# Norm, logits and choice of two routed feed-forwards made chunk by chunk inside the self-attentions in front

## Chip, cores, metric

The kernel runs on 1 core of one Trainium2 chip. The metric is the device time of one execution in microseconds (us), the median over runs.

## The reference

A Perceiver-like network of four layers, each of cross-attention, self-attention and feed-forward on x (128 x 32 tokens of 128 channels, float32), `x = x + f(layernorm(x))` each. Three feed-forwards are mixtures of 8 experts. Those that matter here, cut:

```python
# layer 1 (c_moe): two experts a token, capacity 1280, exact gelu
logits = xt @ w_g;  top_v, top_i = top_k(logits, 2);  probs = softmax over the two
rank = cumsum of the choices over all first choices, then all second ones
h = gelu(x_e @ c_fc[e]);  out = sum over the two of probs * (rank < cap) * (h @ c_proj[e])
# layer 3 (u_moe): one expert a token, behind the attention inside the same sublayer
x = x + attention(rmsnorm(x));  h2 = rmsnorm(x);  top1 = argmax(h2 @ Wr + br)
u = h2 @ W1[e] + b1[e];  y = (u1 * sigmoid(u2)) @ W2[e] + b2[e];  return x + y
```

## The kernel before, in words

X (or `inner`) holds all 4096 tokens in SBUF as 32 tiles of 128 tokens; a chunk is 4 tiles (TPC), there are 8 (CHUNKS). Each sublayer is a block of five instruction streams (SP, POOL, TensorE, ScalarE, VectorE) written out by hand, with semaphores between them and a barrier at its end; only then does the next block's SP fetch its weights.

`self_attention` walks steps s. Step s does the scores of tile s, the weighted values of tile s-2, and work of a chunk at a fixed place: `chunk_at(s, place)` is the chunk c with s = 4c + place. c_self does a cross-attention (s = 0..31) and a self-attention (32..63) in one block of 64 tiles; u_self has 32 tiles with rotary embeddings and a norm of queries and keys (powers at place -3). PSUM bank T_BANK holds a tile's turned weights, O_BANK its outputs. Chunk c of X is ready (`add`, L793) at s = 4c + 9; the base (bias, L407) is added on POOL at 4c + 5.

`routed_experts` is c_moe and u_moe (and a_moe, in layer 0). Its front, for all 32 tiles in two halves: statistics (VectorE), deviation (POOL, L1474), apply (ScalarE, L1653, 4 rows a chunk), turn and logits (TensorE, L1522, L1530), choice and places (VectorE, from L1317), then `put`: POOL scatters each tile's rows by an indirect DMA (L1491) into a DRAM buffer ordered by expert (`slots`), K rows a token. Then SP loads 3 expert tiles at a time (x_slots), TensorE turns them (L1592) and runs `up` (L1606), `turn_hidden` (L1614), `down` (L1623); SP stores the results and POOL gathers them (L1502), VectorE combining (L1907). The second half is scattered during the loop, one transfer a tile. c_moe leaves the combining of its second half to the cross-attention behind (e_cross: gather L2249, combine L2554, four a turn of eight batches in the first eight of 16 turns). Capacity ranks and, in u_moe, `X + base` (L1837) are computed before the loop.

## Time and profile before

| | us |
|---|---|
| median of 3 runs (lowest, highest) | 4197.6 (4193.25, 4206.71) |
| profiled execution: time, span | 4199.95, 4198.1 |
| TensorE, VectorE, ScalarE, POOL busy | 3526.1, 2777.6, 2386.5, 2482.7 |
| mean granted TensorE clock | 0.919 of full |

Busy time is the sum over all sublayers; each has a limit of its own, so the stretches further down matter more. A timeline row gives the start, the length, the engine, the line, output and input, and in brackets the idle time before it and who ended it.

### The profile page before, as it was taken

The numbers are of one execution on the slowest core, as the hardware profiler recorded it, in microseconds if no ns is written. First come the engines' busy times: TensorE is split into PE (matmuls) and PEld (weight loads), VectorE is DVE, ScalarE is ACT, GpSimd is POOL, SyncE is SP. The second block draws the span as 40 slices with busy tenths as digits, with TensorE's granted clock in tenths as the row PEclk, the third lists the DMA queues.
The fourth block names the chain that finished last, engine by engine and source line by source line (L and its number), as shares of the span: only waits on it lengthen the run. The fifth ranks groups of instructions, "written<-read, shape, count | busy, mean of one in ns | idle before, by whom it ended". The sixth has DMA issues, their size and how long they took to land. (4 is left out here: it accounts for less than half of the span.)

```text
span 4198.1 us, 119554 instructions
## 1 busy us (share of the span) xinstructions
PE 3526.1 (84%) x44673; PEld 2462.6 (59%) x44674; DVE 2777.6 (66%) x6958; ACT 2386.5 (57%) x5931; POOL 2482.7 (59%) x2841
## 2 busy tenths in 40 slices
PE   7999959999999759798498999988589999786866
PEld 5666636666666547455366666654356666453444
DVE  6888856666666433477344998876778888663655
ACT  6777725555555424277223777764567777553633
POOL 6666656666666543466433777655456666755733
PEclk9999979999999869889699999998689999887968
DMA  2101010000000112100122111110011011000023
GB/s 69 37 32 37 27 66 5 7 10 10 5 7 2 48 54 77 50 29 24 62 74 64 41 40 40 33 53 17 2 38 37 32 37 32 2 2 6 2 83 94
DMA packets 90544, 145.87 MB, mean 35 GB/s; under 512 B 10112, under 2 KB 66816, under 8 KB 89664
## 3 DMA queue, kind: packets, MB, share of 16 engines
q1 hardware_dynamic: 79936, 119.72, 8.9%
q0 software_dynamic: 10240, 20.99, 1.6%
q8 instruction: 261, 4.28, 0.4%
q14 instruction: 107, 0.88, 0.1%
HBM read 109.61 MB, written 31.06 MB: 34 GB/s over the span
## 5 line engine op out<-in xcount | busy, mean ns | idle before, releaser
L2230 POOL TENSOR_TENSOR t_cross_E<-t_cross_E,t_cross_inverse 128x1028 f32<-128x1028 f32 x128 | 243.4, 1902 | 165.2 <-DVE t_cross_inverse L2512 165.2
L2230 POOL TENSOR_TENSOR a_cross_E<-a_cross_E,a_cross_inverse 128x1028 f32<-128x1028 f32 x128 | 243.3, 1901 | 157.4 <-DVE a_cross_inverse L2512 157.4
L2230 POOL TENSOR_TENSOR e_cross_E<-e_cross_E,e_cross_inverse 128x1028 f32<-128x1028 f32 x128 | 243.6, 1903 | 138.1 <-DVE e_cross_inverse L2512 137.7
L3063 PE MATMUL l_psum<-l_ffn_w,l_hidden 128*128 128x128 f32 x1536 | 218.1, 285 | 32.3 <-POOL l_hidden L2936 32.2
L3063 PEld LDWEIGHTS l_psum<-l_ffn_w,l_hidden 128*128 128x128 f32 x1536 | 190.7, 192 | 70.6 <-POOL l_hidden L2936 43.7
L3056 PE MATMUL l_psum<-l_hT,l_ffn_w 128*128 128x512 f32 x384 | 204.4, 635 | 1.0 <-ACT l_hT L3120 0.9
L2500 DVE TENSOR_REDUCE t_cross_negtop<-t_cross_psum 128x2 f32<-128x514 f32 x256 | 165.5, 688 | 50.0 <-PE t_cross_psum L2314 48.4
L2500 DVE TENSOR_REDUCE a_cross_negtop<-a_cross_psum 128x2 f32<-128x514 f32 x256 | 165.2, 687 | 40.2 <-PE a_cross_psum L2309 39.5
L2500 DVE TENSOR_REDUCE e_cross_negtop<-e_cross_psum 128x2 f32<-128x514 f32 x256 | 164.9, 685 | 37.4 <-PE e_cross_psum L2309 36.7
L2936 POOL TENSOR_TENSOR l_hidden<-l_hidden,l_less 128x512 f32<-128x512 f32 x96 | 122.2, 1295 | 93.3 <-ACT l_hidden L3144 93.3
L3217 DVE TENSOR_TENSOR inner<-l_psum,inner 128x512 f32<-128x512 f32 x48 | 33.2, 692 | 213.0 <-PE l_psum L3048 213.0
L2915 POOL TENSOR_SCALAR l_normed<-inner,l_moments,l_rstd 128x128 f32<-128x128 f32 x192 | 160.3, 845 | 14.8 <-POOL l_rstd L2909 14.8
L2926 POOL TENSOR_TENSOR l_q<-l_q,l_q_stat 128x512 f32<-128x512 f32 x48 | 50.8, 1059 | 183.5 <-DVE l_q_stat L3197 183.5
L2367 PE MATMUL e_cross_psum<-const_sb,e_cross_E 128*128 128x128 f32 x1024 | 135.4, 276 | 2.7 <-POOL e_cross_E L2230 2.1
L2367 PE MATMUL t_cross_psum<-const_sb,t_cross_E 128*128 128x128 f32 x1024 | 134.6, 275 | 2.1 <-POOL t_cross_E L2230 2.1
L2367 PE MATMUL a_cross_psum<-const_sb,a_cross_E 128*128 128x128 f32 x1024 | 133.9, 274 | 2.2 <-POOL a_cross_E L2230 2.1
L2435 ACT ACTIVATE t_cross_kT<-t_cross_psum,t_cross_weights 128x257 f32<-128x257 f32 x128 | 61.1, 477 | 127.4 <-PE t_cross_psum L2293 127.4
L3040 PEld LDWEIGHTS l_psum<-l_qT,l_ctx 32*32 32x32 f32 x6144 | 65.5, 107 | 115.6 <-issue 109.9
L2435 ACT ACTIVATE e_cross_kT<-e_cross_psum,e_cross_weights 128x257 f32<-128x257 f32 x128 | 61.0, 477 | 122.6 <-PE e_cross_psum L2293 122.6
L2435 ACT ACTIVATE a_cross_kT<-a_cross_psum,a_cross_weights 128x257 f32<-128x257 f32 x128 | 61.0, 477 | 120.9 <-PE a_cross_psum L2293 120.9
L2452 ACT ACTIVATE e_cross_E<-e_cross_psum,e_cross_negtop 128x257 f32<-128x257 f32 x256 | 118.8, 473 | 13.4 <-DVE e_cross_negtop L2500 13.2
L2367 PEld LDWEIGHTS e_cross_psum<-const_sb,e_cross_E 128*128 128x128 f32 x1024 | 116.6, 143 | 5.8 <-POOL e_cross_E L2230 2.7
(757 smaller groups left out, 11811.4 us busy)
## 6 DMA issues: line engine op xcount, KB each, us to landing
a_cross_context<-context SPq DMA_DIRECT2D x32, 546.0 KB, 3.5
e_cross_context<-context SPq DMA_DIRECT2D x32, 546.0 KB, 3.5
t_cross_context<-context SPq DMA_DIRECT2D x32, 546.0 KB, 3.5
u_moe_weights<-pack_u_moe SPq DMA_DIRECT2D x1, 5633.0 KB
slots<-l_blank SPq DMA_DIRECT2D x6, 832.0 KB, 12.1
a_moe_x_slots<-slots SPq DMA_DIRECT2D x26, 192.0 KB
slots<-a_moe_y_slots SPq DMA_DIRECT2D x26, 192.0 KB
c_moe_x_slots<-slots SPq DMA_DIRECT2D x26, 192.0 KB
```

Source lines behind the costliest of these rows:

```text
L2230: pool.tensor_tensor(E[:, n % N], E[:, n % N], spread(inverse[:, n % 4], SK, 2), ALU.mult).then_inc(s_unit, 1)
L2367: last = pe.transpose(psum[:, (T_BANK, K_BANK)[c], g * P:(g + 1) * P], E[:, n % N, g, c * P:(c + 1) * P], ident)
L2435: act.activation(kT[:, n % 2], psum[:, K_BANK, 0:SK], ACT.Identity, bias=w("bk")).then_inc(s_k, 1)
L2452: act.activation(E[:, n % N, g], psum[:, g, 0:SK], ACT.Exp, bias=negtop[:, n % 2, g:g + 1], accum_out=total[:, n % 2, g:g + 1]).then_inc(s ...
L2500: dve.tensor_reduce(negtop[:, n % 2, at], psum[:, at, 0:SK], AX.X, ALU.max, negate=True).then_inc(s_top, 1)
L2915: last = pool.tensor_scalar(Y1[:, t], c.tile(t), moments[:, 0, t, 0:1], rstd[:, 0, 1, t:t + 1], ALU.subtract, ALU.mult)
L2926: pool.tensor_tensor(groups, groups, spread(q_stat[:, 2], DH, 2), ALU.mult).then_inc(s_soft, 1)
L2936: pool.tensor_tensor(hidden[:, f], hidden[:, f], less[:, f - 2], ALU.add).then_inc(s_late, 1)
L3040: last = pe.matmul(psum[rows, C_BANK, b * S:(b + 1) * S], ctx[rows, b], qT[rows, b * S:(b + 1) * S], start=True, stop=True)
L3056: pe.matmul(psum[:, U_BANKS[f % 2]], c.ffn(f * P), hT2[:], start=True, stop=True).then_inc(s_up, 1)
L3063: last = pe.matmul(psum[:, D_BANK, t * P:(t + 1) * P], hidden[:, f, t * P:(t + 1) * P], c.ffn((NF + f) * P), start=(f == 0 and t == 0), st ...
L3217: dve.tensor_tensor(c.chunk(), tiles(psum[:, C_BANK]), c.chunk(), ALU.add).then_inc(s_mid, 1)
```

## The change

For c_moe and u_moe, norm, logits and choice (new class `Front`, on data in `Choice`) of chunks 0 to 6 move into the self-attention in front (c_self, u_self), at places 9 to 14 behind each chunk. There the first part's places are computed too, and POOL scatters it: 12 tiles (24 transfers) in c_self, 16 in u_self. Those attentions run four steps longer. The routed block then begins with the experts of the first part; chunk 7, the second part's choice and scatters, the ranks (in 14 pieces) and the base's addition (in 8) are made between expert tiles. c_moe's parts are 12 and 20 tiles (11 and 16 triples of expert tiles, before 13 and 13), so e_cross combines 40 results instead of 32. a_moe uses the same classes with its order kept. The bodies of `choose` and `places` are those of before, cut in pieces. The core of the diff:

```diff
+        F_STATS, F_DEVIATION, F_APPLY, F_TURN, F_LOGITS = 9, 10, 11, 13, 14
+        LOGITS = slice(G * J * (DH + 1), G * J * (DH + 1) + TPC * 8)
+        if choice:
+            front = Front(sc, choice, 0, 0)
+            CHOOSE = (ALL_CHUNKS - CHUNKS) * TPC + choice.cut[1] - TPC + F_LOGITS
+            TALLY = CHOOSE + choice.K + 1
+            PUT = max(TALLY + 2, ALL_TILES - 3)
+            TALLIES = slice(LOGITS.stop, 512)
+            TRANSFERS = choice.cut[1] * choice.K
+            for s in range(-STATS, ALL_TILES + (10 if choice else 6)):
                 step(s)
+        def fronted(s, place):
+            c = chunk_at(s, place) if choice else None
+            c = None if c is None else c - (ALL_CHUNKS - CHUNKS)
+            return c if c is not None and 0 <= c < CHUNKS - 1 else None
+        def put_at(s):
+            if not choice or s < PUT:
+                return range(0)
+            slow = max(ALL_TILES - 2 - PUT, 0)
+            if s < PUT + slow:
+                return range(s - PUT, s - PUT + 1)
+            per = -(-(TRANSFERS - slow) // 4)
+            first = slow + (s - PUT - slow) * per
+            return range(min(first, TRANSFERS), min(first + per, TRANSFERS))
...
                 fetch(sp)
+            if choice:
+                front.fetch(sp)
...
+                c = fronted(s, F_DEVIATION)
+                if c is not None:
+                    front.deviation(pool, link, c)
+                for n in put_at(s):
+                    if n == 0:
+                        pool.wait_ge(front.s_place, 1)
+                    front.put(pool, slots, 0, n)
...
+                c = fronted(s + 1, F_TURN)
+                if c is not None:
+                    pe.wait_ge(front.s_fT, c + 1)
...
+                if s >= 2:
+                    pe.wait_ge(s_ET, min(s - 1, ALL_TILES))
+            def outputs_free(s):
+                if s >= 3:
+                    pe.wait_ge(s_O, min(s - 2, ALL_TILES))
...
+                c = fronted(s, F_TURN)
+                if c is not None:
+                    turned_free(s)
+                    front.turn(pe, c, psum[:, T_BANK])
+                c = fronted(s, F_LOGITS)
+                if c is not None:
+                    front.arrived(pe)
+                    outputs_free(s)
+                    if c > 0:
+                        pe.wait_ge(front.s_read, c)
+                    front.logits(pe, c, psum[:, O_BANK, LOGITS])
+                if choice and s == TALLY:
+                    outputs_free(s)
+                    front.tallies(pe, 0, psum[:, O_BANK, TALLIES])
...
+                c = fronted(s, F_TURN)
+                if c is not None and rotary:
+                    front.turned(act, c, psum[:, T_BANK])
...
+                    c = fronted(s, F_APPLY)
+                    if c is not None:
+                        if c == 0:
+                            front.arrived(act)
+                        front.apply(act, c)
...
+                c = fronted(s, F_TURN)
+                if c is not None:
+                    front.turned(act, c, psum[:, T_BANK])
...
+                c = fronted(s, F_LOGITS)
+                if c is not None:
+                    if c == 0:
+                        front.arrived(dve)
+                    front.read_logits(dve, (c,), psum[:, O_BANK, LOGITS])
+                if choice and s == TALLY:
+                    front.places(dve, link, 0, 0, psum[:, O_BANK, TALLIES])
                 if tile_exists(s - 2):
                     unit(s - 2)
+                if choice and 0 <= s - CHOOSE < choice.K:
+                    front.choose(dve, link, 0, s - CHOOSE)
+                if choice and 0 < s - TALLY < 3:
+                    front.places(dve, link, 0, s - TALLY, psum[:, O_BANK, TALLIES])
+                c = fronted(s, F_STATS)
+                if c is not None:
+                    dve.wait_ge(s_done, c + ALL_CHUNKS - CHUNKS + 1)
+                    front.statistics(dve, c)
...
+class Front:
...
+            eng.wait_ge(self.s_router, 16)
+    def statistics(self, dve, c):
+        k, n, at = self.choice, c - self.c0, slice(c * TPC, (c + 1) * TPC)
+        for t in range(c * TPC, (c + 1) * TPC):
+            last = dve.bn_stats(k.stats[:, t], k.source[:, t])
+        last.then_inc(self.s_stats, 1)
+        dve.wait_ge(self.s_stats, n + 1)
+        for t in range(c * TPC, (c + 1) * TPC):
+            last = dve.bn_aggr(k.moments[:, t], k.stats[:, t])
+        last.then_inc(self.s_moments, 1)
+        if k.rms:
+            dve.wait_ge(self.s_moments, n + 1)
+            dve.tensor_tensor(k.square[:, at], k.moments[:, at, 0], k.moments[:, at, 0], ALU.mult).then_inc(self.s_square, 1)
+            dve.wait_ge(self.s_square, 2 * n + 1)
+            dve.tensor_tensor(k.square[:, at], k.square[:, at], k.moments[:, at, 1], ALU.add).then_inc(self.s_square, 1)
...
+    def deviation(self, pool, link, c):
...
+    def apply(self, act, c):
+        k = self.choice
+        act.wait_ge(self.s_factor, c - self.c0 + 1)
+        for t in range(c * TPC, (c + 1) * TPC):
+            last = act.activation(k.rows[:, t], k.source[:, t], ACT.Identity, bias=0.0 if k.rms else k.shift[:, t:t + 1],
+                                  scale=k.factor[:, t:t + 1])
+        last.then_inc(self.s_norm, 1)
+    def turn(self, pe, c, bank):
+        k = self.choice
+        pe.wait_ge(self.s_norm, c - self.c0 + 1)
+        for n in range(TPC):
+            last = pe.transpose(bank[:, n * P:(n + 1) * P], k.rows[:, c * TPC + n], k.core.const("ident"))
+        last.then_inc(self.s_turned, 1)
+    def turned(self, act, c, bank):
+        k, n = self.choice, c - self.c0
+        act.wait_ge(self.s_turned, n + 1)
+        if k.hT_all is None and n >= 2:
+            act.wait_ge(self.s_logits, n - 1)
+        act.activation(k.chunk_out(c), bank, ACT.Identity, bias=k.w("ln_b") if k.affine else 0.0,
+                       scale=k.w("ln_w") if k.affine else 1.0).then_inc(self.s_fT, 1)
+    def logits(self, pe, c, out):
+        k = self.choice
+        pe.wait_ge(self.s_fT, c - self.c0 + 1)
+        mine = k.chunk_out(c)
+        for n in range(TPC):
+            last = pe.matmul(out[:, n * k.E:(n + 1) * k.E], mine[:, n * P:(n + 1) * P], k.w("router"), start=True, stop=True)
+        last.then_inc(self.s_logits, 1)
+    def read_logits(self, dve, chunks, source):
+        k, tiles = self.choice, slice(chunks[0] * TPC, chunks[-1] * TPC + TPC)
+        dve.wait_ge(self.s_logits, chunks[-1] - self.c0 + 1)
+        self.reads += 1
+        dve.tensor_tensor(k.l[:, tiles], source.rearrange("p (t e) -> p t e", e=k.E),
+                          spread(k.w("router_b"), len(chunks) * TPC, 1), ALU.add).then_inc(self.s_read, 1)
+        dve.wait_ge(self.s_read, self.reads)
...
+    def tallies(self, pe, g, out):
+        k = self.choice
+        width = k.E * k.width(g)
+        pe.wait_ge(self.s_mask, g - self.g0 + 1)
+        mask = (k.one if k.K == 1 else k.p8)[:, k.tiles(g)].rearrange("p t e -> p (t e)")
+        for n, table in enumerate(("upto", "ones")):
+            last = pe.matmul(out[:, n * width:(n + 1) * width], k.core.const(table), mask, start=True, stop=True)
+        last.then_inc(self.s_count, 1)
...
+    def put(self, pool, slots, g, n):
+        k = self.choice
+        t = k.cut[g] + n // k.K
+        pool.indirect_dma_start(slots.halves[g], bass.IndirectOffsetOnAxis(ap=k.place_i[:, n % k.K, t:t + 1], axis=0),
+                                k.rows[:, t], None).then_inc(slots.s_put[g], 16)
...
+def routed_experts(core, name, slots, kind, nf, choice, begun=False, base=None, store_out=None, behind=False):
...
+    LOGIT_BANK, COUNT_BANK, RANK_BANK = 2, 4, 3
+    RANKING = 7
...
+        PLACES_AT = 6 if K == 2 else 4
+        PUT_AT = PLACES_AT + 2
+        RANK_AT = PLACES_AT + 6
...
             def put(g):
-                pool.wait_ge(s_place, g + 1)
-                for t in range(HALF):
-                    if g == 0 and t in (4, 8):
-                        deviation(PART + 1 + t // 4)
+                pool.wait_ge(front.s_place, g - front.g0 + 1)
+                transfers = choice.width(g) * K
+                for n in range(transfers):
+                    if g == 0 and n in (4 * K, 8 * K):
+                        front.deviation(pool, link, PART + 1 + n // (4 * K))
+                    if g == 1:
+                        pool.wait_ge(s_down, PUT_AT + n * (ONE - 6 - PUT_AT) // transfers if begun else n + 1)
+                    front.put(pool, slots, g, n)
...
+            if begun:
+                front.deviation(pool, link, LAST)
+            else:
+                for c in range(PART + 2):
+                    front.deviation(pool, link, c)
+                put(0)
...
             up(0)
+            if begun:
+                front.turn(pe, LAST, psum[:, RANK_BANK])
...
+                if i % LOT == LOT - 3:
                     load_owners(i // LOT + 1)
                 turn_hidden(i)
+                if begun and i == 1:
+                    front.logits(pe, LAST, psum[:, COUNT_BANK, 0:TPC * E])
+                if begun and i == PLACES_AT - 1:
+                    front.tallies(pe, 1, psum[:, COUNT_BANK, TPC * E:])
+                if capacity and i == RANK_AT:
+                    pe.wait_ge(front.s_owner, 2 - front.g0)
+                    ranks()
...
             x_out(0)
+            if begun:
+                front.apply(act, LAST)
...
+                if begun and i == 0:
+                    front.turned(act, LAST, psum[:, RANK_BANK])
+                if begun and K == 2 and i == RANK_AT:
+                    ratios()
...
+            def beside(i):
+                if i == 2:
+                    front.read_logits(dve, (LAST,), psum[:, COUNT_BANK, 0:TPC * E])
+                if 2 <= i < 2 + K:
+                    front.choose(dve, link, 1, i - 2)
+                if 0 <= i - PLACES_AT < 3:
+                    front.places(dve, link, 1, i - PLACES_AT, psum[:, COUNT_BANK, TPC * E:])
+                if K == 2 and i == RANK_AT - 2:
+                    apart()
...
+            def add_base(c):
+                at = slice(c * TPC, (c + 1) * TPC)
+                dve.tensor_tensor(X[:, at], X[:, at], base[:, at], ALU.add).then_inc(s_base, 1)
...
+                if begun:
+                    beside(i)
+                if capacity and 0 <= i - RANK_AT - 2 < 2 * RANKING:
+                    ranking(*divmod(i - RANK_AT - 2, RANKING))
+                if base is not None and 0 <= i - RANK_AT < CHUNKS:
+                    add_base(i - RANK_AT)
+                if i >= ONE + 6 and taken < cut[1] * K:
                     combine(taken)
                     taken += 1
...
+        FETCHES = 2 * (TILES - left.cut[1]) if behind else 0
...
             def fetch_result(m):
-                t, k = TILES // 2 + m // 2, m % 2
...
+            with Scope(core, "u_choice") as sc:
+                choice = Choice(sc, "u_router", "top1", inner, hT_rows, "eps6", rms=True)
+                self_attention(core, "u_self", r8, ("u_self",), causals=(True,), second=("eps6", True), keep=inner,
+                               rotary=("rcos", "rsin"), choice=choice, slots=slots)
+                routed_experts(core, "u_moe", slots, "glu", 2, choice, begun=True, base=inner, store_out=store_out)
...
+        def second_self():
+            with Scope(core, "c_choice") as sc:
+                choice = Choice(sc, "c_router", "capacity", X, hT_rows, "eps5", affine=False, first=12)
+                self_attention(core, "c_self", r8, ("c_cross", "c_self"), (context32, None), (True, False), choice=choice, slots=slots)
+                routed_experts(core, "c_moe", slots, "gelu", 4, choice, begun=True, behind=True)
+                cross("e_cross", r8, behind=(choice, slots))
```

## Rows read from the trace of the kernel before

**Rows 1.** Busy time by stretch (header names the columns): c_self, c_moe's loop, u_moe's loop.
```profile
core 0: us, PE busy (x) PEld busy (x) DVE busy (x) ACT busy (x) POOL busy (x), PEclk, DMA share, GB/s
1885.00:1975.00 90.00, 86.70 (x2425) 54.51 (x2424) 71.52 (x192) 75.01 (x140) 64.63 (x82) 1.00 0.02 4
2074.00:2277.00 203.00, 195.49 (x1167) 136.75 (x1167) 85.04 (x188) 60.45 (x105) 61.05 (x64) 0.99 0.23 67
4072.00:4168.00 96.00, 87.71 (x430) 57.05 (x429) 65.70 (x161) 43.46 (x113) 30.57 (x32) 0.95 0.27 78
```

**Rows 2.** Timeline: weights' issue, first transpose of gathered rows; start, length, engine, line, idle before.
```profile
1987.68 0.43 SPq L157 DMA_DIRECT2D c_moe_weights<-pack_c_moe  x1
...
2072.83 0.87 PE L1592 MATMUL c_moe_psum<-const_sb,c_moe_x_slots 128*128 128x128 f32 x3 [18.77 <-issue]
...
4020.97 0.42 SPq L157 DMA_DIRECT2D u_moe_weights<-pack_u_moe  x1
...
4071.13 0.87 PE L1592 MATMUL u_moe_psum<-const_sb,u_moe_x_slots 128*128 128x128 f32 x3 [6.22 <-issue]
```

**Rows 3.** DMA issue (KB, us to landing); busy times 4036 to 4040, last figures DMA share, GB/s.
```profile
c_moe_weights<-pack_c_moe SPq DMA_DIRECT2D x1, 4096.0 KB, 12.3
...
u_moe_weights<-pack_u_moe SPq DMA_DIRECT2D x1, 5633.0 KB
...
4036.00:4040.00 4.00, 2.00 (x9) 2.00 (x10) 2.43 (x8) 0.00 (x0) 0.00 (x0) 0.50 0.00 0
```

**Rows 4.** POOL's timeline in c_moe's front: scatters.
```profile
2022.39 0.96 POOL L1491 DMA_INDIRECT slots<-hT_all,behind_place_i  x1 [0.30 <-issue]
2023.65 0.96 POOL L1491 DMA_INDIRECT slots<-hT_all,behind_place_i  x1 [0.30 <-issue]
...
2026.69 1.04 POOL L1491 DMA_INDIRECT slots<-hT_all,behind_place_i  x1 [0.16 <-issue]
```

**Rows 5.** Timeline: c_self's last bases on POOL, last scores in c_self and u_self.
```profile
1972.64 2.49 POOL L407 TENSOR_TENSOR X<-X,c_self_bo 128x512 f32<-128x512 f32 x2
...
1976.55 0.53 PE L453 MATMUL c_self_psum<-c_self_k_heads,c_self_qT 32*32 32x128 f32 x32
...
4005.78 0.51 PE L453 MATMUL u_self_psum<-u_self_k_heads,u_self_qT 32*32 32x128 f32 x32
```

**Rows 6.** Timeline: one cycle of c_self; last row from c_moe's front.
```profile
1949.41 0.60 PE L467 MATMUL c_self_psum<-const_sb,c_self_normed 128*128 128x128 f32 x4
...
1949.53 1.06 POOL L401 TENSOR_TENSOR c_self_k_heads<-c_self_kT,const_sb 128x512 f32<-128x512 f32 x1
...
1950.81 0.30 PEld L477 LDWEIGHTS c_self_psum<-c_self_hT,c_self_weights 128*128 128x128 f32 x2 [0.20 <-ACT c_self_hT L587]
...
1959.46 1.16 PE L552 MATMUL c_self_psum<-c_self_weights,c_self_aT 128*128 128x128 f32 x8
...
1961.85 0.30 PEld L477 LDWEIGHTS c_self_psum<-c_self_hT,c_self_weights 128*128 128x128 f32 x2 [0.20 <-ACT c_self_hT L587]
...
1994.44 1.64 ACT L1653 ACTIVATE hT_all<-X,c_moe_shift,c_moe_factor 128x128 f32<-128x128 f32 x4
```

**Rows 7.** Timeline: u_self's keys, waiting for the turned norm.
```profile
3973.35 1.13 PE L477 MATMUL u_self_psum<-u_self_hT,u_self_weights 128*128 128x512 f32 x2 [2.23 <-ACT u_self_hT L587]
```

**Rows 8.** VectorE's timeline in c_moe's front: choice and places of 16 tiles.
```profile
2004.14 0.29 DVE L1317 TENSOR_REDUCE c_moe_best<-c_moe_l 128x16 f32<-128x128 f32 x1
...
2008.36 0.29 DVE L1734 TENSOR_TENSOR c_moe_p<-c_moe_one,c_moe_two 128x128 f32<-128x128 f32 x1
...
2015.76 0.18 DVE L1796 CAST c_moe_owner_i<-c_moe_owner 128x39 int32<-128x39 f32 x1
```

**Rows 9.** Combining by tile (min/median/max), POOL's multiplications, e_cross's maxima in two stretches.
```profile
L1907 DVE SCALAR_TENSOR_TENSOR X<-behind_got,behind_part,X x32: 341/344/344, 2194.0 to 2272.4; 128x128 f32<-128x128 f32 x32
...
L2554 DVE SCALAR_TENSOR_TENSOR X<-behind_got,behind_part,X x32: 959/1390/2002, 2310.7 to 2570.9; 128x128 f32<-128x128 f32 x32
...
L2230 POOL TENSOR_TENSOR e_cross_E<-e_cross_E,e_cross_inverse 128x1028 f32<-128x1028 f32 x128 | 243.6, 1903 | 138.1 <-DVE e_cross_inverse L2512 137.7
...
2316.00:2551.00 235.00, 71.26 (x111) 98.07 (x336) 1.00 0.14 42
2551.00:2787.00 236.00, 76.74 (x120) 103.14 (x354) 1.00 0.12 36
```

More of the change, by code:

```diff
@@ L836, in step @@
                             rotate(c, n)
+            link = Link(dve, front.s_link, 0) if choice else None
             steps(step)
@@ L1345, in routed_experts @@
-def routed_experts(core, name, router, rows, slots, kind, choice, nf, source, eps, rms=False, twice=False, capacity=None,
-                   base=None, hT_all=None, store_out=None, behind=None):
-    nc, X = core.nc, core.X
-    E, K, HALF = 8, (1 if choice == "top1" else 2), TILES // 2
-    NT = core.half_tiles[K]
-    TRIPLES = -(-NT // 3)
-    COUNT, LOT = 2 * 3 * TRIPLES, 16
-    halves = kind in ("silu", "glu")
-    width = nf * P * (2 if halves else 1)
+        self.s_put, self.puts = [ctx.enter_context(nc.semaphore(f"put{g}")) for g in range(2)], [0, 0]
@@ new lines, in __init__ @@
+        self.s_got, self.gots = [ctx.enter_context(nc.semaphore(f"got{n}")) for n in range(4)], 0
+def routed_experts(core, name, slots, kind, nf, choice, begun=False, base=None, store_out=None, behind=False):
+    nc, X = core.nc, core.X
+    E, K, cut, rows, hT_all = choice.E, choice.K, choice.cut, choice.rows, choice.hT_all
+    TRIPLES, COUNT, LOT = sum(choice.triples), choice.count, 16
+    ONE = 3 * choice.triples[0]
+    capacity = 1280 if choice.kind == "capacity" else None
+    width = nf * P * (2 if kind in ("silu", "glu") else 1)
@@ L1580, in load_owners @@
                 if first < last:
+                    if begun and first < ONE < last:
+                        pe.wait_ge(front.s_owner, 1)
                     at = lot % 2 * LOT
@@ L1857, in load_owners @@
                 if first < last:
+                    if begun and first < ONE < last:
+                        dve.wait_ge(front.s_owner, 1)
                     at = lot % 2 * LOT
@@ L2586, in cross_attention @@
         if behind:
[L2587 removed]
+            slots.gots = gots + 16 * FETCHES // 4
         sc.close_block()
```

532 lines of the change are left out of this document (263 added, 269 removed).

## The prediction

> **What bounds the kernel now.** I read the busy time by stretch first. The program is twelve sublayers one behind another, each closed by a barrier, so each must be costed alone; the page's averages say little. The self-attention in front of the third feed-forward (c_self) has TensorE busy for 86.7 us of 90, ScalarE 75.0, VectorE 71.5; the expert loop of c_moe has TensorE 195.5 of 203; that of u_moe has VectorE 65.7 of 96 beside TensorE's 87.7 [rows 1]. Then the timeline of the two routed sublayers' starts: from the issue of the expert weights to the first transpose of gathered rows, 2072.83 - 1987.68 = 85.2 us pass in c_moe and 4071.13 - 4020.97 = 50.2 us in u_moe [rows 2]. In these fronts norm, logits, choice and 32 (16) scatters follow one another; nothing of them is hidden. They are what the change attacks.
>
> **What is saved, and what comes up behind it.** The weights' transfer starts behind the same barrier as before. It took 12.3 us for 4096 KB, and u_moe's 5633 KB were in by 4036, when the DMA share is 0: 15.0 us [rows 3]. The first loads of x queue behind them on SP; 768 KB at 4096 KB in 12.3 us are 2.3 us. So the loops start 14.6 and 17.3 us after the issue: saved 85.2 - 14.6 = 70.6 and 50.2 - 17.3 = 32.9, together **103.5 us**. This is nearly certain (the first load alone lets transposes begin, at best 1.7 us earlier in each).
>
> **What is added, five terms.**
> (1) *Tail of c_self.* Chunk 6 of the front has its statistics at s=65, its deviation on POOL at s=66, and there 24 scatters stand ahead of it: one at s=61, then 6, 6, 6, 5. POOL issues one scatter per 1.26 us, and scatter with deviation takes 3.04, so a deviation 1.8 [rows 4]. POOL is free of bases 14 and 15 at 1975.1, before the last scores at 1976.55 [rows 5], so its queue starts full: the deviation of chunk 5 waits for the VectorE of s=61 and ends about with the last scores' start; then 23 x 1.26 = 29.0, base(15) 1.25, deviation 1.8, ScalarE's four rows 1.64 [rows 6], and transposes, copy, logits and read at the low clock (TensorE's twice the durations of term 3) about 1.2 + 0.7 + 1.8 + 0.4, barrier 0.9: 38.7 us from the last scores to the weights' issue. Before it was 1987.68 - 1976.55 = 11.1 [rows 2, 5]. Cost **27.6 us**; behind POOL stands only this, and the barrier waits for it.
> (2) *Tail of u_self.* 16 scatters at s=30..33, deviation 1.35 (no shift), base 1.25, apply 1.3: 20.2 + 1.25 + 1.35 + 1.3 + 4.9 = 29.0 against 4020.97 - 4005.78 = 15.2 [rows 2, 5]. Cost **13.8 us**.
> (3) *Steady part of c_self.* A cycle of four tiles takes 1961.85 - 1950.81 = 11.04 us. Four transposes are 0.60 us at full clock, eight matmuls with a 128-column weight load 1.16 (logits 0.97) [rows 6]: 1.5 us on a full TensorE, three chunks wholly and two partly, 6 us. ScalarE's four rows (1.64) stand ahead of values_out, and behind that is the turned norm on which the keys wait: the keys at 1950.81 follow its copy after 0.2 us of wait [rows 6]. That is 1.6 us late for four chunks, 6 us. The choice: 14 operations from 2004.14 to 2008.65, and the whole with places to 2015.94 [rows 8], some 10 us of VectorE for 12 tiles in s=54..59, where own statistics have ended; with 4 us of slack left, 6.5. Sum **18.5 us**. From below: TensorE's 6 and 2 for the choice, 8; from above 30.
> (4) *Steady part of u_self.* In the rotary step the front's copy stands ahead of the powers in ScalarE's queue and waits for four transposes: 1.9 us later for the turned norm, on which the keys already wait 2.23 us [rows 7]. Rows' apply before values_out adds 1.3, less what idle time takes: 3.3 us for each of four chunks, 13.2, and 4.3 for the choice in light steps: **17.5 us**, between 8 and 28.
> (5) *The loops.* c_moe has 81 expert tiles for 78 (11 + 16 triples for 26), 203 / 78 = 2.6 us with the start, 2.5 in the loop: 7.5. TensorE's last chunk, tallies and ranks: 3.3. VectorE has 85.0 of 203 us busy [rows 1], but a piece over 1.5 us delays the copy of hT, and down waits: two pieces of choice, one of places, two rank ends, and two loads of ScalarE's tables around the ratios: 6.2. **17.0 us** (12 to 24). u_moe: choice 2.0, places 5.3 and base 4.6 are 11.9 us on VectorE, whose slack is (96 - 65.7) / 48 = 0.6 us a tile less the waits in its chain, so of 12 pieces some 6 us stay, and TensorE's extra work 1.5: **7.5 us** (3 to 13). The base's addition, now in eight pieces, is inside. e_cross takes 40 results for 32: two more turns of the kind with fetches. 111 maxima in 235 us against 120 in 236 [rows 9] are 33.9 and 31.5 us a turn (16 each): **4.7 us** (0 to 5).
>
> New waits and who stands behind them: TensorE's turn(s-1) waits for the front's copy out of the same bank; weighted(s-2) and the two output transposes (0.9 us) lie between, about as long as ScalarE needs for keys_out and that copy, so nothing. VectorE's read of the logits waits for matmuls that stand ahead of weighted in TensorE's queue, so they are there. VectorE's places wait for the tallies, 0.5 us, and unit(s-2) behind them; that is in the 6.5. The front's statistics at s=4c+9 follow the add of the same chunk in the same queue: 1.3 us at the end of a step, taken up by the next two, whose TensorE work (keys and queries) is longest. The router's load, 8 KB, is issued at the attention's start, some 100 us ahead of its use.
>
> a_moe keeps its order. Scatters of c_moe's second part need 40 x 1.26 = 50 us from tile 8 on, done near tile 28; the load that needs them is used at tile 31. Nothing, unless late by more than 7 us.
>
> Costs: 27.6 + 13.8 + 18.5 + 17.5 + 17.0 + 7.5 + 4.7 = 106.6, against 103.5. The profiled execution took 4199.95 us (span 4198.1), so 4203.1; the runs' median 4197.6 is 2.4 below it: **4201 us**. What leaves the fronts comes back in the attentions, mostly because POOL's scatters are put where nothing else is left to hide them.
>
> **A rule against the change.** In e_cross a VectorE operation with two SBUF operands, L2554, took 1390 ns (median); the same work in c_moe, where POOL only gathers, at most 344 [rows 9]. So beside POOL's 1.9 us multiplications [rows 9] it waits some 1.05 us. In c_self POOL runs multiplications of 1.06 us [rows 6], and 16 of the choice's operations have two SBUF operands; in u_self 10. The Trainium skill, SBUF — State Buffer (section "SBUF: two separate sides"), says that VectorE with two SBUF inputs and a GpSimd operation lock each other out for a whole instruction. By that rule, the trace agrees; it would move the sum as the second rival does.
>
> **Rivals.**
> *Absorbed, faster.* The slack in the attentions takes the stalls: (3) 8, (4) 9, the loops 13 and 4, e_cross 3, the tails as above: 78.4 against 103.5, 25 us gained: 4173. For it: engines are late at different steps and catch up. Against: c_self's TensorE has 3 us idle in 90, and u_self's powers lie on its chain. It decides once the stalls of (3) to (5) are under 48 us together (I have 65).
> *Port wait, slower.* Each of 26 operations waits 0.58 us (1.05 of 1.9, scaled to 1.06): 15 us on a VectorE that has no slack there: 4216. Against: in c_self existing two-operand work is rare, so no row shows the wait there, and POOL is busy only 64.6 of 90 us. It decides from 0.4 us a wait.
> *Late second part, slower.* If the 40 scatters or the pieces in c_moe are later than reckoned, SP stands at the load and stores queue behind it; six tiles of 2.5 us and more: 4216 to 4236.
>
> **Chances.** My sum 0.35 (4187 to 4210); absorbed 0.33; port wait 0.20; late part or heavier queues 0.12. Within 0.3% (12.6 us, about what a measurement here can tell) 0.35, faster 0.33, slower 0.32. Range 4162 to 4236: below, the absorbed case with the 3.4 us of the first loads, e_cross's last 3 and 5 more of the loops; above, the late part short of its end. What is left out is about 1 in 10 on each side.
>
> **What would show it.** First gathered transpose 14 to 16 us behind c_moe's weights' issue (17 in u_moe); in c_self from last scores to that issue 38 us, 24 scatters in a row with TensorE idle; a cycle of 13 to 14 us instead of 11.04 from tile 43 on; u_self's cycle 3 us longer; 81 tiles; choice operations of 0.3 us, or 0.6 and more if the port decides. Wrong would make it: scatters beside the scores instead of behind them, or a weights' wait much over 15 us.

## The result: 4235.5 us against 4198.4, slower by 0.9%, and the profile after

The changed kernel takes 4235.54 us (median of 4 runs, 4230.52 to 4240.82), the kernel before 4198.39 beside it: 1.0087 of it, 95% interval 1.0066 to 1.0107. The forecast was 4201, no change within 0.3%; the interval excludes that. 4235.54 is inside the range 4162 to 4236 by half a microsecond, at the end that the rival *late second part* had set. So it went the way of the "slower" rivals, and the question is by what.

The profiled execution took 4234.88 us, its span is 4233.0. The first line of its page (engine, busy us, share of the span, instructions) shows hardly more work than before, 5.4 us for TensorE and 14.1 for VectorE over 3526.1 and 2777.6, so most of the 34.9 us by which the span grew is waiting:

```profile
PE 3531.5 (83%) x44718; PEld 2462.5 (58%) x44719; DVE 2791.7 (66%) x6989; ACT 2388.8 (56%) x5937; POOL 2480.5 (59%) x2841
```

The same marks as in [rows 2, 5] give the stages. Timeline of the changed kernel: two scores of c_self four tiles apart, the last scores, the weights' issue, and the first transpose of gathered rows, in c_self/c_moe and then u_self/u_moe:

```profile
1928.64 0.50 PE L496 MATMUL c_self_psum<-c_self_k_heads,c_self_qT 32*32 32x128 f32 x32
1942.77 0.50 PE L496 MATMUL c_self_psum<-c_self_k_heads,c_self_qT 32*32 32x128 f32 x32
1995.64 0.51 PE L496 MATMUL c_self_psum<-c_self_k_heads,c_self_qT 32*32 32x128 f32 x32 [0.31 <-DVE c_self_E L861]
2041.79 0.33 SPq L158 DMA_DIRECT2D c_moe_weights<-pack_c_moe  x1
2055.06 0.87 PE L1863 MATMUL c_moe_psum<-const_sb,c_moe_x_slots 128*128 128x128 f32 x3 [13.99 <-DMA c_moe_x_slots<-slots]
...
4039.41 0.74 PE L496 MATMUL u_self_psum<-u_self_k_heads,u_self_qT 32*32 32x128 f32 x32 [2.73 <-DVE u_self_E L861]
4081.18 0.33 SPq L158 DMA_DIRECT2D u_moe_weights<-pack_u_moe  x1
4098.20 0.87 PE L1863 MATMUL u_moe_psum<-const_sb,u_moe_x_slots 128*128 128x128 f32 x3 [17.73 <-DMA u_moe_x_slots<-slots]
```

Worked out in the same way for both kernels (differences of the starts of such rows, each sublayer from the issue of its weights, the columns in us):

| stage | before | changed | difference | forecast |
|---|---|---|---|---|
| c_self, to the last scores | 193.6 | 212.7 | +19.1 | +18.5 |
| its tail, to c_moe's weights | 11.1 | 46.1 | +35.0 | +27.6 |
| c_moe, weights to first transpose | 85.2 | 13.3 | -71.9 | -70.6 |
| c_moe, the rest | 206.3 | 233.5 | +27.2 | +17.0 |
| e_cross | 545.3 | 547.7 | +2.4 | +4.7 |
| retention to t_cross, and all before c_self | 2766.3 | 2765.5 | -0.8 | 0 |
| u_self, to the last scores | 198.0 | 220.5 | +22.5 | +17.5 |
| its tail, to u_moe's weights | 15.2 | 41.8 | +26.6 | +13.8 |
| u_moe, weights to first transpose | 50.2 | 17.0 | -33.2 | -32.9 |
| u_moe, the rest | 127.0 | 134.8 | +7.8 | +7.5 |

The savings came as forecast. Four costs are larger: the two tails by 7.4 and 12.8, c_moe's rest by 10.2, u_self by 5.0.

Timeline of c_self's tail in the changed kernel, where the forecast had everything wait for POOL's scatters alone:

```profile
1996.33 1.05 POOL L1652 DMA_INDIRECT slots<-hT_all,c_choice_place_i  x1 [0.17 <-issue]
...
2003.62 0.26 DVE L868 RECIPROCAL c_self_inverse<-c_self_psum 128x16 f32<-128x16 f32 x1 [4.53 <-issue]
...
2006.46 0.60 ACT L690 ACTIVATE c_self_ET<-c_self_psum 128x512 f32<-128x512 f32 x1 [6.71 <-remote]
2006.96 1.64 ACT L1537 ACTIVATE hT_all<-X,c_choice_shift,c_choice_factor 128x128 f32<-128x128 f32 x4
2007.12 0.71 PE L575 MATMUL c_self_psum<-v_own,c_self_ET 128*32 128x36 f32 x32 [8.10 <-ACT c_self_ET L690]
...
2016.36 0.59 PE L560 MATMUL c_self_psum<-const_sb,c_self_E 128*128 128x128 f32 x2 [2.13 <-issue]
...
2025.38 0.96 POOL L1652 DMA_INDIRECT slots<-hT_all,c_choice_place_i  x1 [0.30 <-issue]
2029.15 0.26 DVE L868 RECIPROCAL c_self_inverse<-c_self_psum 128x16 f32<-128x16 f32 x1 [24.95 <-remote]
2029.30 0.60 ACT L690 ACTIVATE c_self_ET<-c_self_psum 128x512 f32<-128x512 f32 x1 [20.71 <-remote]
...
2029.95 1.12 PE L1546 MATMUL c_self_psum<-const_sb,hT_all 128*128 128x128 f32 x4 [13.01 <-ACT c_self_ET L690]
```

The scatters stand 1.26 us apart, as reckoned. But VectorE's reciprocal at 2029.15 reads what TensorE's L575 wrote at 2007.12 to 2007.83: 21 us lie between a matmul's end and its reader, and the reader has nothing else to do. ScalarE's copy at 2029.30 (L690) waits for the transposes of 2016.36 to 2016.95. Both go on only behind the last scatter, which POOL issued at 2025.38. The view of waits over this stretch (engine, tile and line, whom it waited for, us, times, longest) finds no instruction of the core that released them and writes "remote". One engine tells another that it is done by incrementing a semaphore; below, a late signal means that the reader went on long after the instruction it waited for had ended.

```profile
ACT c_self_ET L690 <- remote: 27.4, 2, 20.7
DVE c_self_inverse L868 <- remote: 24.9, 1, 24.9
```

In the prediction's account the work of the last tiles ends early, and only chunk 6's deviation waits for POOL. Here that work waits in the middle of itself, and chunk 6's statistics, ready only at 2033.55, then let the deviation start 7.3 us after POOL was done with the last scatter.

### The profile page after: what moved, and what is told of

It reads as the page before. It is cut to its first block and busy times, and to the rows that moved or that the text cites. A ratio compares the mean times of both kernels' runs of the same rounds, so it can differ in the third digit from the quotient of the medians.

```text
span 4233.0 us, 119710 instructions
## 1 busy us (share of the span) xinstructions
PE 3531.5 (83%) x44718; PEld 2462.5 (58%) x44719; DVE 2791.7 (66%) x6989; ACT 2388.8 (56%) x5937; POOL 2480.5 (59%) x2841
## 5 line engine op out<-in xcount | busy, mean ns | idle before, releaser
L3315 PE MATMUL l_psum<-l_ffn_w,l_hidden 128*128 128x128 f32 x1536 | 218.6, 286 | 33.0 <-POOL l_hidden L3188 32.9
L3315 PEld LDWEIGHTS l_psum<-l_ffn_w,l_hidden 128*128 128x128 f32 x1536 | 191.0, 192 | 70.6 <-POOL l_hidden L3188 44.2
L3469 DVE TENSOR_TENSOR inner<-l_psum,inner 128x512 f32<-128x512 f32 x48 | 33.2, 692 | 213.0 <-PE l_psum L3300 213.0
L1894 PEld LDWEIGHTS c_moe_psum<-c_moe_weights,c_moe_hT 128*128 128x128 f32 x648 | 79.3, 191 | 78.2 <-issue 78.2
```

The source lines that it names most:

```text
L1894: last = pe.matmul(psum[:, D_BANK + i % 2, 0:P], hT[:, i % 2, f * P:(f + 1) * P], down_of[:, at, f * P:(f + 1) * P].rearrange("p a c -> p ...
L3315: last = pe.matmul(psum[:, D_BANK, t * P:(t + 1) * P], hidden[:, f, t * P:(t + 1) * P], c.ffn((NF + f) * P), start=(f == 0 and t == 0), st ...
```

## The experiments

Four sets of kernels were run; the kernels of one set ran on one chip beside the kernel before, at 4181.7, 4193.7, 4185.0 and 4189.5 us in the four sets. Ratios are to the kernel before of the same set, with 95% intervals; loops, tails and starts are read from one profiled execution each.

### Set 1: what is moved, what is burst

`fronts_back`: attentions as before, norm and choice at the start of each block, both first parts 16 tiles; the ranks and the base in pieces in the loop, as in the changed kernel.

```diff
-                choice = Choice(sc, "c_router", "capacity", X, hT_rows, "eps5", affine=False, first=12)
-                self_attention(core, "c_self", r8, ("c_cross", "c_self"), (context32, None), (True, False), choice=choice, slots=slots)
-                routed_experts(core, "c_moe", slots, "gelu", 4, choice, begun=True, behind=True)
+                choice = Choice(sc, "c_router", "capacity", X, hT_rows, "eps5", affine=False)
+                self_attention(core, "c_self", r8, ("c_cross", "c_self"), (context32, None), (True, False))
+                routed_experts(core, "c_moe", slots, "gelu", 4, choice, behind=True)
```

(and the same for u_self and u_moe)

> The changed kernel with norm, logits and choice of c_moe and u_moe put back to the start of their own blocks (16 + 16 tiles, attentions as before); ranks in 14 pieces and the base's addition in 8 pieces stay in the loop. Theory (the attentions and their tails are what the change costs, each added term as the stage table shows): both attentions take their old 204 and 213 us; c_moe starts its loop about 9 us earlier than before (the ranks stood ahead of it), u_moe about 5 us, and the pieces in the loops give some 5 us back: 4190 us, between 4182 and 4198. Rival (the loop's pieces are the dear part): the c_moe loop takes 15 us or more over the 206 of before and the time is over 4203.

Measured 4181.29 against 4181.73, 0.9995 (0.9985 to 1.0005): no change. c_moe starts after 75.1 us (83.3 in the old block of `burst_before`, same set), as expected; u_moe after 50.7, so the expected 5 us are not there: POOL's scatters end its start, not the base's addition. Its c_moe loop takes 208.2 us, 1.3 more than there. The rival falls. Of the expected 8 us the profiled execution shows 5.8 against that of `burst_before` (spans 4175.0 and 4180.8), the median of ten runs 0.4 against the kernel before, which I take.

`scatters_after`: the changed kernel, scatters moved to the routed block's start.

```diff
-            if not choice or s < PUT:
+            if True:
...
             if begun:
                 front.deviation(pool, link, LAST)
+                for n in range(choice.width(0) * K):
+                    front.put(pool, slots, 0, n)
```

> The changed kernel, the first part's 24 and 16 scatters issued at the start of the routed block, beside the weights' transfer, and not at the attention's end. Theory 1 (the burst of scatters holds up TensorE, ScalarE and VectorE at the attention's end): from last scores to the weights' issue 22 us in c_self (46.2 with the burst) and 24 in u_self (41.8); loops begin 37 and 27 us behind the weights' issue; sum about 4227 us. Rival (the longer chain of the last chunk is what costs, the scatters lie beside it): tails stay over 32 us, 4245 us or more.

Measured 4198.83, 1.0036 (1.0024 to 1.0049). Starts 37.4 and 27.2 us, as theory 1 had them; tails 17.1 and 21.0, 5 and 3 us shorter than it had; c_moe's loop 220.6, with code that took 233.5 in the changed kernel. The rival falls: the scatters cost the tails, not the last chunk's longer chain. This run can't tell POOL's queue from late signals, since both leave the tail with the scatters, and the time is below the expected 4227 (1.0068) also because c_moe's loop was 12.9 us quicker.

`one_in_flight`: the changed kernel, each scatter in the attentions' tails issued once the one before has landed.

```diff
                     if n == 0:
                         pool.wait_ge(front.s_place, 1)
+                    else:
+                        pool.wait_ge(slots.s_put[0], slots.puts[0] + 16 * n)
```

> The changed kernel, each scatter in the attentions' tails issued only when the one before it has landed. Theory 1a (several scatters in flight are what delays TensorE's signals): VectorE's reciprocals and ScalarE's copies follow their matmuls within 0.5 us also beside the scatters; POOL takes about 3 us a scatter, so 72 and 48 us, and the time is about 4300. Theory 1b (any scatter delays them): the same delays of 5 to 20 us between matmul and reader as with the burst.

One run, 4238.93 us, for about 4300 expected. A scatter took 2.5 us, not 3, so the tails are 66.5 and 47.3 us, not 72 and 48. VectorE's reciprocals followed their matmuls at once: of the 24.9 us above nothing is left in the same view.

```profile
ACT hT_all L1539 <- POOL c_choice_shift L1532: 50.1, 1, 50.1
DVE c_self_inverse L870 <- PE c_self_psum L577: 2.8, 2, 1.5
```

`burst_before`: the old kernel with a burst in c_moe's loop.

```diff
-                            pool.wait_ge(s_down, t * K + k + 1)
+                            pool.wait_ge(s_down, 1 if name == "c_moe" else t * K + k + 1)
```

> The kernel before, with c_moe's second 32 scatters issued back to back from the first expert tile on, instead of one a tile; nothing else. Theory (a burst beside a working TensorE delays it): the c_moe loop takes 10 to 25 us longer than its 206, 4208 to 4223 us, with waits of 1 to 5 us of ScalarE and VectorE for matmuls that have ended. Rival (the pieces of choice, places and ranks cause the 20 us of stalls in the changed kernel's c_moe loop): no change, 4198 us.

1.0000 (0.9990 to 1.0009), loop 206.9 us for an expected 216 to 231: the rival's number. This did not fit the tails, and the 220.6 and 222.1 us of c_moe's loop in this set did not fit the 233.5. Either a burst alone is innocent, or it was in this set.

### Set 2: the changed kernel once more, and two variants

> The changed kernel as it stands, once more, beside the other kernels of this set and on their chip. Its first profile has 46 and 41 us from last scores to weights' issue and a c_moe loop of 233.5 us, with waits of 2 to 21 us of VectorE and ScalarE for matmuls that had ended; the kernel without scatters in the attentions' tails had 17, 21 and 220.6 us. Theory 1 (the burst beside a working TensorE does it, always): tails 44 to 47 and 40 to 43 us again, 36 us slower than the kernel before. Rival (the waits belong to that one execution or chip): tails of 39 and 30 us as my sum had them, loop 221 us, 15 to 20 us slower.

1.0112 (1.0094 to 1.0130), tails 46.2 and 40.8 us, loop 232.2: it repeats.

`powers_first`: u_self's step in ScalarE.

```diff
-                c = fronted(s, F_TURN)
-                if c is not None and rotary:
-                    front.turned(act, c, psum[:, T_BANK])
...
                         values_out(c, 0)
                         values_out(c, 1)
+                    c = fronted(s, F_TURN)
+                    if c is not None:
+                        front.turned(act, c, psum[:, T_BANK])
                     if tile_exists(s):
                         exponential(s)
```

> The changed kernel, in u_self's steps ScalarE's copy of the front's transposes behind the powers, the copy of the turned norm and the values, not ahead of them. Theory (term 4: the copy ahead of the powers delays the keys by 1.9 us a chunk): u_self to its last scores 220.8 us becomes 211 to 216, the whole 5 to 9 us faster than the changed kernel. Rival (TensorE's next transposes wait for the copy, so that a late copy costs as much): 220 us, or more.

u_self to its last scores 212.2 us against 220.7 of the run beside it, 8.5 us less, so the theory holds; the medians are 4227.1 and 4238.6. TensorE's keys wait for the turned norm 5.3 us less. TensorE's waits in u_self, of the changed kernel and then of this one:

```profile
PE u_self_psum L520 <- ACT u_self_hT L656: 18.2, 6, 3.6
PE u_self_psum L560 <- ACT u_self_square L705: 11.7, 6, 2.3
```

```profile
PE u_self_psum L520 <- ACT u_self_hT L656: 12.9, 6, 2.8
PE u_self_psum L560 <- ACT u_self_square L705: 11.7, 6, 2.3
```

`u_twelve`: `fronts_back` with u_moe's first part of 12 tiles, and its second 20 scatters back to back beside the loop.

```diff
-                choice = Choice(sc, "u_router", "top1", inner, hT_rows, "eps6", rms=True)
+                choice = Choice(sc, "u_router", "top1", inner, hT_rows, "eps6", rms=True, first=12)
...
-                        pool.wait_ge(s_down, PUT_AT + n * (ONE - 6 - PUT_AT) // transfers if begun else n + 1)
+                        pool.wait_ge(s_down, PUT_AT + n * (ONE - 6 - PUT_AT) // transfers if begun else n + 1 if K == 2 else 1)
```

> Fronts put back as in that run, and in u_moe a first part of 12 tiles with the 20 scatters of the second issued back to back from the first expert tile (48 expert tiles, as before). Theory (the start of a routed block is POOL's scatters, 1.26 us each): 4 scatters less, u_moe's start 50.7 becomes 45.6 us, its loop within 1 us: 5 us faster than the kernel before, 4177 where that has 4182. Rival (the burst beside the loop holds TensorE up): the loop of u_moe 5 us longer, no gain.

1.0062 (1.0048 to 1.0077), slower where 5 us of gain were expected. The start did not shrink (50.9 us): with fewer scatters the second choice on VectorE, to 4059.97, was last. And the loop took 154.4 us for 125.1 in `fronts_back`: the rival, and over five times its price. The edit also changes the parts to 12 and 20 tiles; but the sixth result already comes 20.7 us later behind the first transpose than in `fronts_back` (37.5 us for 16.8), with the burst right before it (8.9 to 32.9), and the last of the 48 is 24.4 us late. In the same execution c_moe's loop, whose scatters stand one to an expert tile, took 209.5 us (208.2 in `fronts_back`). The attentions are those of before, so the front in them is not needed for the waits. In u_moe's loop, a result, a hidden tile and the next matmuls:

```profile
4077.51 0.29 DVE L2137 TENSOR_TENSOR u_moe_y_slots<-u_moe_psum,u_moe_weights 128x128 f32<-128x128 f32 x1 [2.52 <-DMA c_moe_x_slots<-slots]
4078.11 0.38 ACT L1975 ACTIVATE u_moe_hT<-u_moe_psum 128x256 f32<-128x256 f32 x1 [3.88 <-DMA c_moe_x_slots<-slots]
...
4086.78 0.29 DVE L2137 TENSOR_TENSOR u_moe_y_slots<-u_moe_psum,u_moe_weights 128x128 f32<-128x128 f32 x1 [4.99 <-DMA c_moe_x_slots<-slots]
...
4090.88 0.38 ACT L1975 ACTIVATE u_moe_hT<-u_moe_psum 128x256 f32<-128x256 f32 x1 [12.11 <-DMA c_moe_x_slots<-slots]
...
4091.43 1.22 PE L1894 MATMUL u_moe_psum<-u_moe_weights,u_moe_hT 128*128 x4 [9.61 <-issue]
```

### Set 3: three kernels on one chip

> The changed kernel again, now on one chip with the two kernels it is to be compared with. Theory 1 (its bursts beside a working TensorE hold up the signals, on any chip): from last scores to weights' issue 46 and 41 us, c_moe's loop 233 us. Rival (chips differ: the set in which the burst in the old kernel's loop did nothing ran on a chip that shows no such waits): whatever this chip shows, the three kernels show it together.

> The kernel before with c_moe's second 32 scatters back to back, again. If chips differ (rival), then where the changed kernel has its 46 us tails this kernel's c_moe loop is 10 to 25 us over 206; if it is 207 here too beside tails of 46 us, then a burst alone does not do it and something of the changed kernel is needed as well.

> The changed kernel with the first scatters at the routed block's start, again, same chip as the two others. Theory 1: tails of 17 and 21 us, starts of 37 and 27 us, 20 us faster than the changed kernel. Its c_moe loop, whose code is that of the changed kernel: 221 us as the first time if the loop's waits come from what the attention's end left behind, 233 us if they belong to the chip.

The rival holds so far that the three kernels agree within their set: none shows a late signal. Theory 1, on any chip, falls. Here the changed kernel takes 1.0026 of the kernel before (1.0015 to 1.0036; 4196.70 against 4184.97), the burst in the old loop 0.9990 (0.9980 to 1.0000), the scatters at the block's start 1.0043 (1.0029 to 1.0057), 5 us slower than the changed kernel where 20 us faster were expected: its tails are 20.1 and 7.3 us shorter (18.6 and 21.8), its starts 24.2 and 9.9 us longer (37.4 and 27.3), its c_moe loop 222.5. Without late signals the scatters cost a little more in front of the routed blocks than in the tails. The tails of the changed kernel are 38.7 and 29.0 us, the numbers of the prediction to the tenth, and c_moe's loop is 221.1. The reciprocal after the same matmul starts 0.1 us behind it, beside the same burst, and the long wait is that for POOL's base:

```profile
1991.30 0.71 PE L575 MATMUL c_self_psum<-v_own,c_self_ET 128*32 128x36 f32 x32 [1.50 <-ACT c_self_ET L690]
...
1992.07 0.26 DVE L868 RECIPROCAL c_self_inverse<-c_self_psum 128x16 f32<-128x16 f32 x1 [1.49 <-PE c_self_psum L575]
...
2010.90 1.27 POOL L442 TENSOR_TENSOR X<-X,c_self_bo 128x512 f32<-128x512 f32 x1
...
2012.30 0.69 DVE L878 TENSOR_TENSOR X<-c_self_psum,X 128x512 f32<-128x512 f32 x1 [13.15 <-POOL X L442]
...
2017.41 0.96 POOL L1652 DMA_INDIRECT slots<-hT_all,c_choice_place_i  x1 [0.30 <-issue]
2018.39 0.21 POOL L1525 TENSOR_TENSOR c_choice_var<-c_choice_moments,const_sb 128x4 f32<-128x4 f32 x1
```

### Set 4: both kinds of burst, and a paced tail in the same execution

`one_in_flight` can't tell what a paced tail does where a burst delays, since its set may have been free of the waits with a burst too. So `burst_and_paced`, on top of `powers_first`, paces u_self alone:

```diff
                     if n == 0:
                         pool.wait_ge(front.s_place, 1)
+                    elif rotary:
+                        pool.wait_ge(slots.s_put[0], slots.puts[0] + 16 * n)
```

and `bursts_in_loops` is the kernel before with

```diff
-                            pool.wait_ge(s_down, t * K + k + 1)
+                            pool.wait_ge(s_down, 1 if name != "a_moe" else t * K + k + 1)
```

> The changed kernel with the powers ahead of the front's copy in u_self, c_self's 24 scatters in a burst as they were, and u_self's 16 each issued when the one before has landed. So far two chips showed waits of 5 to 21 us for matmuls that had ended, beside the burst, and tails of 46 and 41 us; one chip showed none and tails of 38.5 and 28.7. Theory (bursts hold up the signals, on some chips only): where c_self's tail is 46 us, u_self's paced tail shows no such wait and is POOL's time alone, 16 x 2.5 + 7 = 47 us, as on the chip of the first paced run; where c_self's tail is 38.5, u_self's is 47 too. Rival (on those chips any scatter beside TensorE does it): the paced tail takes 50 us or more with waits of 2 us and more for ended matmuls. The powers: u_self to its last scores 8 us less than 221 to 225 on any chip.

> The kernel before with the second scatters of c_moe (32) and u_moe (16) back to back from the first expert tile on. Theory: on a chip where c_self's burst gives a tail of 46 us, c_moe's loop is 10 us or more over 206 and u_moe's 10 us or more over 126; on a chip with a tail of 38.5 both are as before. Rival (only the new kernels are touched): 206 and 126 on either.

In this set the waits were there. (Its chip bears the same number as that of set 3; whether it is the same chip at another time, I can't tell.) `burst_and_paced`: 1.0106 (1.0086 to 1.0127, two runs); c_self's tail 45.1 us with the waits, u_self's paced tail 47.5, POOL's time alone, as the theory had it. One execution, c_self's tail and then u_self's:

```profile
DVE c_self_inverse L870 <- remote: 29.3, 2, 24.8
ACT c_self_ET L692 <- remote: 27.2, 2, 20.6
```

```profile
ACT hT_all L1539 <- POOL u_choice_factor L1528: 26.7, 1, 26.7
...
POOL slots L1654 <- DMA slots<-hT_all,u_choice_place_i: 23.2, 15, 2.9
...
DVE u_self_inverse L870 <- PE u_self_psum L577: 2.9, 3, 1.5
```

u_self to its last scores took 212.1 us again. `bursts_in_loops`: 1.0124 (1.0107 to 1.0141), no better than the changed kernel, though nothing in it differs from the kernel before but two bounds of a wait: c_moe's loop 243.0 us for 206.3, u_moe's 142.2 for 127.0. Its theory holds and its rival, that only the new kernels are touched, falls. The loss lies inside the burst: c_moe's fifth result comes 50.6 us behind the first transpose for 18.4, the burst lasts until 47.5, and from the eighth on a result takes 2.5 us as before. The waits from 2080 to 2130:

```profile
ACT c_moe_hidden L1705 <- remote: 34.9, 3, 23.3
DVE c_moe_y_slots L1897 <- remote: 30.2, 2, 23.1
```

Busy times of one stretch of 40 us with the burst in it, here and then in `burst_before` of set 1, the same code in c_moe:

```profile
core 0: us, PE busy (x) PEld busy (x) DVE busy (x) ACT busy (x) POOL busy (x), PEclk, DMA share, GB/s
2067.00:2107.00 40.00, 20.02 (x86) 12.31 (x86) 4.62 (x9) 6.93 (x11) 24.90 (x26) 0.76 0.16 56
```

```profile
core 0: us, PE busy (x) PEld busy (x) DVE busy (x) ACT busy (x) POOL busy (x), PEclk, DMA share, GB/s
2067.00:2107.00 40.00, 39.09 (x237) 27.39 (x236) 15.68 (x32) 11.79 (x21) 29.45 (x31) 1.00 0.31 99
```

TensorE worked 20.0 us of 40 in the one and 39.1 in the other; POOL issued its scatters 1.26 us apart in both (27 and 31 of the 32 fall into the stretch), and the transfers' share of the DMA engines is half as large where TensorE stands.

## Where the forecast held and where it failed, by its steps

**What bounds the kernel; what is saved.** Right: starts of 13.3 and 17.0 us against 14.6 and 17.3. The savings are 105.0 us for 103.5.

**Terms 1 and 2, the tails.** The mechanism is right: POOL's queue of scatters stands ahead of chunk 6's deviation and the barrier behind that. Where no signal was late (set 3) the tails are 38.7 and 29.0 us, as summed; the deviation starts 30.6 us behind the last scores (1987.79 to 2018.39), for 29.0 + 1.25 in the sum. Moving the scatters to the block's start leaves 17 to 19 and 21 to 22 us. What was missing: in three of the five comparisons (the first, sets 2 and 4) a burst also holds up the other engines, 7.4 and 12.8 us more in the first profile.

**Term 3, c_self.** Forecast 18.5, measured 19.1, but the first 30 tiles, which the change doesn't touch, were 4.6 us quicker than before in that execution; a cycle of four tiles takes 1942.77 - 1928.64 = 14.1 us for 11.04, at the end of the 13 to 14 forecast, and tiles 30 to 63 take 23.7 us more (113.7 for 90.0). I had charged four chunks with ScalarE's delay; there are five with a front that meet running tiles. Set 3, whose kernels agree in the first 30 tiles, has 21.9 us (211.03 for 189.15 in `same_chip_burst`).

**Term 4, u_self.** 22.5 (26.3 in set 3) for 17.5: mis-sized, inside its bounds. The front's copy ahead of the powers, put at 1.9 us a chunk (7.6 for four), is worth 8.5 by `powers_first`; where the other 4 to 8 us come from stays open.

**Term 5, the loops.** u_moe 7.8 for 7.5 (6.2 in set 3). c_moe 27.2 for 17.0 with late signals, 14.5 without (221.1 against 206.6 in set 3). The 40 scatters in c_moe's loop are a burst too, from 31.0 to 80.5 us behind the first transpose in set 3, 1.27 us apart on average; so late signals can reach this loop. e_cross 2.4 for 4.7 (3.5 in set 3).

**The sum.** In set 3 the change costs 11.7 us, 1.0026, inside the 0.3% that the forecast called no change; the forecast had 3.4. In the first comparison it costs 37.2 us, and that this lay inside the range is luck: the upper end was set by a rival with another mechanism. The step that failed is the sentence that in the tails "behind POOL stands only this", and with it the costing of a scatter at its 1.26 us of POOL and nothing else. With late signals the tails cost 35.0 and 26.6 us for 27.6 and 13.8, and c_moe's loop 27.2 for 17.0. The trace of before could not warn of it, since it never has a burst beside a dense stream of matmuls: in its fronts the scatters stand back to back [rows 4], but the other engines are nearly idle, and in its loops each scatter waits for an expert tile.

**The rivals.** *Port wait*: the wait is there, its size is not. Of the choice's operations in c_self three were long, the others at their usual length; the last row is one of those:

```profile
L1616 DVE TENSOR_TENSOR c_choice_ahead<-c_choice_upto,c_choice_counts 128x96 f32<-128x96 f32 x1 | 1.1, 1072 | 0.0
L1616 DVE TENSOR_TENSOR c_choice_first_tile<-c_choice_tiles_upto,c_choice_tiles_of 128x8 f32<-128x8 f32 x1 | 1.0, 973 | 0.0
L1422 DVE TENSOR_TENSOR c_choice_one<-c_choice_cand,c_choice_best 128x96 f32<-128x96 f32 x1 | 0.9, 910 | 0.0
...
L1422 DVE TENSOR_TENSOR c_choice_two<-c_choice_cand,c_choice_best 128x96 f32<-128x96 f32 x1 | 0.3, 258 | 0.0
```

That is 0.8 + 0.8 + 0.65 = 2.3 us, and in u_self two waited 0.7 and 0.4 us; the rival had 15 us for the 26. Each of the three began 0.1 to 0.3 us into a POOL multiplication of 1.06 us and ended 0.02 to 0.12 us behind it. The rule of the Trainium skill (SBUF — State Buffer, section "SBUF: two separate sides"), that the one of the two that starts first has the port for its whole instruction, fits these three. It is worth little here, since POOL's multiplications seldom meet the choice. *Absorbed*: it did not happen; c_self cost 19.1 us and u_self 22.5, for 8 and 9 in that rival. *Late second part, slower*: the time is in its range and its mechanism is not: the lateness is in the signals, not in SP's queue.

**A version that beats both** was not found. `fronts_back` equals the kernel before in set 1; it was not run beside the changed kernel. Where signals are prompt (set 3) the changed kernel is 0.26% slower than the kernel before, and moving the scatters to the block's start makes 0.43%. `powers_first` takes 8.5 us from u_self and leaves the kernel slower (1.0077 beside 1.0112, set 2).

## What to carry to other kernels

Work that moves into another stage takes its queue with it: sum what stands behind the moved instructions on their engine at the moment when they are issued (here 24 scatters ahead of one short chain that the barrier waits for). Spread indirect DMAs over the work beside them, one per expert tile as in the kernel before, rather than issue them back to back beside a working TensorE: c_moe's burst alone cost 37 us in set 4 and nothing in sets 1 and 3 (u_moe's, 15 us in set 4, was not run where signals were prompt). When a profile shows a reader idle long after its matmul ended, run the same kernel on another chip, or again later, before explaining it by its own dependences.

## What was not expected of the hardware

Comparisons of one kernel differ in kind. With the same code, data and nearly the same clock (0.921 and 0.925 granted), readers of TensorE's results beside a burst of indirect DMAs started up to 21 us late in some sets and on time in others, and within a set this happened in every kernel that had a burst beside a working TensorE, or in none. In u_moe's loop of `u_twelve` POOL's sequencer cleared 51 semaphores: 37 of them took 38 ns or less each, and 14, between 4081.6 and 4097.9, about 700 ns each (the last scatter was issued at 4094.17). Such clears, of over 600 ns, stand in all six traces with late signals: 14 there, 21 in `bursts_in_loops`, 2 each in the changed kernel and `burst_and_paced`, 1 each in `changed_again` and `powers_first`. They stand in none of the seven traces of sets 1 and 3, and not in the kernel before, whose longest took 332 ns. The data were not slower: the scatters' packets of 4096 bytes took 194 ns (median) in the changed kernel's late tail and 193 in the prompt one of set 3. That speaks for slow work on semaphores rather than slow data; it goes together with the late signals, and no run changed it alone. What fills that path, and what sets such a set apart, a chip, a time or other work on the chip, stays open. Pacing by landing (2.5 us a scatter) avoids it and gains nothing: the paced tail of u_self is 47.5 us, the burst's 41 to 42. Of the paces between, one is on record: u_moe's loop in the kernel before issues 16 scatters in 27 us, and took 127.0 us in the first comparison, 125.3 and 125.6 with the same code in `burst_before` and `same_chip_burst`.
